# LayerNorm column sums taken from the f32 tile instead of a bf16 copy (gated-scan block, 8 cores)

## What is computed

```
xg    = gelu(x)
for fwd, bwd:                     # the scan runs forwards / backwards in time
    xb = xg @ Wx + bx
    a  = sigmoid(xb @ Wga + bga) * sigmoid(a_logit)
    h  = scan(a, sqrt(1 - a*a) * sigmoid(xb @ Wgx + bgx) * xb)
    y += h @ Wo + bo
r1  = gelu(y/2 + x) @ ld_W + ld_b + x + x
x1  = layernorm(r1)
r2  = x1 + clip((x1 @ sign(W_ffn).T) * scale + bias, -100, 100)
out = layernorm(r2)               # over the 1024 features
```

## Time and profile before

| | us |
|---|---|
| median of 2 runs (757.25 and 760.36) | 758.81 |
| the profiled execution | 756.73 |
| span of its slowest core (core 0) | 755.2 |
| spans of the other cores | 733.6 to 752.3 |
| mean granted TensorE clock of core 0 | 0.939 of 2.4 GHz |

### The profile page before, as it was taken

How to read it: one execution, slowest core, us unless ns; L and a number is a source line. 1 busy time by engine, 2 the same in 40 slices (tenths; PEclk the granted TensorE clock), 3 DMA queues, 4 the chain that set the end, 5 groups by cost and what they waited for, 6 DMA issues and landing times.

```text
span 755.2 us, 7191 instructions; the slowest of 8 cores (733.6 to 755.2 us)
## 1 busy us (share of the span) xinstructions
PE 622.8 (82%) x2667; PEld 263.7 (35%) x2720; DVE 330.6 (44%) x193; ACT 353.6 (47%) x262; POOL 48.7 (6%) x92
## 2 busy tenths in 40 slices
PE   0449999999999999999999979988896798775510
PEld 0014444444444444444444424433332243221100
DVE  0000000005677687677771202032478388475274
ACT  2442332236776877877832201133563467534710
POOL 2010000000000000002032111000000000000000
PEclk9999999999999999999999989999998989887855
DMA  8995000012232222223289999165530000112024
GB/s 186 243 199 98 1 0 1 1 15 33 37 43 42 31 41 43 42 30 55 42 110 195 228 188 183 45 196 187 175 111 1 0 1 1 45 66 112 0 65 158
DMA packets 23218, 61.34 MB, mean 81 GB/s; under 512 B 2704, under 2 KB 2704, under 8 KB 23184
## 3 DMA queue, kind: packets, MB, share of 16 engines
q0 software_dynamic: 12672, 23.07, 21.2%
q1 hardware_dynamic: 8208, 29.42, 12.2%
q10 hardware_dynamic: 2304, 8.39, 3.8%
HBM read 75.55 MB, written 8.39 MB: 111 GB/s over the span
## 4 chain that ended last, share of the span: by engine, by line
PE 64%; DMA 15%; DVE 9%; ACT 6%; issue 4%; SPq 0%; ACTq 0%; DVEq 0%; POOLq 0%
PE psA L152 34%; PE psB L152 30%; DMA A<-x 6%; DMA A<-Wof 3%; DMA A<-Wob 2%; DVE A L719 2%; DMA out<-A 2%; DVE A L783 2%; DMA A<-Wffn 2%; DVE A L712 2%; ACT A L868 1%; DVE A L683 1%; ACT A L778 1%; DVE srows L611 1%; DVE A L690 1%
## 5 line engine op out<-in xcount | busy, mean ns | idle before, releaser
L152 PE MATMUL psA<-A 128*128 128x512 bf16 x1503 | 361.6, 396 | 70.1 <-ACT A L329 22.6
L152 PEld LDWEIGHTS psA<-A 128*128 128x128 bf16 x1536 | 151.4, 100 | 275.4 <-issue 112.4
L152 PE MATMUL psB<-A 128*128 128x512 bf16 x1004 | 226.2, 380 | 1.7 <-DVE A L568 0.6
L152 PEld LDWEIGHTS psB<-A 128*128 128x128 bf16 x1024 | 100.3, 98 | 122.8 <-issue 3.0
L429 DVE TENSOR_SCALAR A<-A,dvec_sb 128x2048 f32<-128x2048 f32 x16 | 20.6, 1286 | 168.8 <-ACT A L425 168.8
L440 DVE TENSOR_TENSOR A<-A 128x2048 f32<-128x2048 f32 x16 | 36.7, 2292 | 51.0 <-ACT A L433 51.0
L573 ACT ACTIVATE A<-A,dvec_sb 128x1024 bf16<-128x1024 f32 x16 | 18.4, 1148 | 75.1 <-DVE A L568 75.1
L425 ACT ACTIVATE A<-psB,vecs_sb 128x2048 f32<-128x2048 f32 x16 | 31.5, 1967 | 32.0 <-PE psB L152 32.0
L152 PE MATMUL psB<-A,ones_sb 128*1 128x512 bf16 x128 | 33.8, 395 | 14.0 <-ACT A L894 11.2
L431 ACT ACTIVATE A<-A 128x2048 f32<-128x2048 f32 x16 | 30.6, 1910 | 23.8 <-DVE A L429 23.8
L568 DVE SCALAR_TENSOR_TENSOR A<-psA,A 128x1024 f32<-128x1024 f32 x8 | 9.8, 1225 | 65.2 <-PE psA L152 37.7
(11 more groups left out here) (54 smaller groups left out, 341.5 us busy)
## 6 DMA issues: line engine op xcount, KB each, us to landing
A<-x SPq DMA_DIRECT2D x40, 512.0 KB, 7.9
A<-x ACTq DMA_DIRECT2D x8, 512.0 KB, 15.3
A<-Wof POOLq DMA_DIRECT2D x16, 256.0 KB, 11.4
A<-Wob POOLq DMA_DIRECT2D x16, 256.0 KB, 13.4
A<-Wffn SPq DMA_DIRECT2D x8, 512.0 KB, 6.1
out<-A ACTq DMA_DIRECT2D x8, 512.0 KB, 4.1
out<-A SPq DMA_DIRECT2D x8, 512.0 KB, 3.9
A<-Wxf POOLq DMA_DIRECT2D x8, 256.0 KB, 31.5
```

The source lines that it names most:

```text
L152: inst = e.matmul(oa, lh, rh, start=st, stop=sp)
```

## The change

In the ffn stage the bf16 copy of r2 is dropped. ACT squares the f32 tile, and the two S1 matmuls of each chunk take the f32 tile as moving operand and a new f32 column of ones as stationary. The squares stay bf16, and so do S2 and the statistics of the ld stage.

```diff
+    ones32_sb = nc.alloc_sbuf_tensor("ones32_sb", [128, 1], F32)
...
+    bd.op("vector", lambda e: e.memset(ones32_sb[:], 1.0), writes=[onesB], inc="dv")
...
-    def stats_tiles(src_ap_fn, src_buf, k, slot):
+    def stats_tiles(src_ap_fn, src_buf, k, slot, f32=False):
+        lh = ones32_sb.ap() if f32 else ones_sb.ap()
         tiles, treads = [], []
         for t in range(2):
-            tiles.append((ones_sb.ap()[:],
-                          src_ap_fn(k, t),
+            tiles.append((lh, src_ap_fn(k, t),
...
         r2B = rA3.new(f"r2h{h}", CH)
-        r2bfB = [new_over(rR1e[k:k + 1], f"r2bfh{h}_{k}") for k in range(CH)]
-        r2bf_ap8 = [A5.ap()[:, R1 // 2 + k * 1024: R1 // 2 + (k + 1) * 1024]
-                    for k in range(CH)]
...
-            bd.op("vector",
-                  lambda e, o=o: e.tensor_copy(r2bf_ap8[o],
-                                               r2f[:, o * 1024:(o + 1) * 1024]),
-                  reads=[r2B[o]], writes=[r2bfB[o]], inc="dv")
-
             def _stats(o=o):
                 sl = o % 2
                 bd.op("scalar",
                       lambda e, o=o, sl=sl:
-                      e.activation(rsq_ap[sl], r2bf_ap8[o], AF.Square),
-                      reads=[r2bfB[o]], writes=[rsqB[sl]], inc="sc")
-                stats_tiles(lambda k, t: r2bf_ap8[k][:, t * 512:(t + 1) * 512],
-                            r2bfB[o], o, 2)
+                      e.activation(rsq_ap[sl], r2f[:, o * 1024:(o + 1) * 1024],
+                                   AF.Square),
+                      reads=[r2B[o]], writes=[rsqB[sl]], inc="sc")
+                stats_tiles(lambda k, t:
+                            r2f[:, k * 1024 + t * 512: k * 1024 + (t + 1) * 512],
+                            r2B[o], o, 2, f32=True)
```

## The result

The changed kernel took 769.83 us (median of 12 runs), the kernel before 758.13 us (median of 10) in the same series. The forecast was 769.3.

A forecast was written before the change was run, and what follows sets the result against it. TensorE was taken to bound the ffn stage's first half and both half-end bursts, DVE's apply steps the second half's first six chunks. +6.1 + 6.25 - 1.8 = +10.5 us on 758.8 gave 769.3 us, range 762 to 784.

The forecast's parts named there:

- The price of an f32 matmul: 32 ones matmuls (S1) in the ffn stage: each four bf16 streams at 2.4 GHz, loads hidden, 0.87 us.
- The bursts: Ones matmuls at each ffn half's end, on which L605 and LayerNorm wait: +6.1 us first half (S(0) included), +6.25 second.
- S(0) of the second half hidden: First chunk's sums in the second half fall into TensorE's 6.45 us wait for ACT's square, so they cost nothing.
- The casts: DVE, second half: three casts off the path before the apply step L712, 3 x 0.61 us, -1.8 us.
- The sum: Both half-end costs less the cast gain: +6.1 + 6.25 - 1.8 = +10.5 us, giving 769.3 us, +1.4%.
- The signs: Profile checks: 32 f32 matmuls of 0.87 us, L605 6 and about 10.5 us later, no 0.6 us step, clock 1.00.
- anything ahead of 626 us moves: Stated failure condition: the prediction is wrong if the profile changes before 626 us, in the ffn stage's first half or earlier.
- The clock in the range: Part of the forecast's own range, 764 to 775: a burst starting at 1.2 instead of 2.4 GHz costs 2 to 3 us.
- The squares from f32, the memset and the new waits at nothing: ACT squares (1048 against 1046 ns), one small DVE memset at 10 us, and waits on finished reads: no cost.
- Exposed loads: Rival, f32 ones matmuls: 83 ns weight load open per stream, 1.20 us per matmul, +20.3 us, 779.1; chance 0.13.
- The fallen clock: Rival, both half-end bursts: TensorE runs at 1.2 GHz during f32 work, +34.7 us, 793.5; chance 0.10.
- Fewer passes: Rival, f32 ones matmuls: each costs one or two bf16 streams, 757.0 or 759.6 us; chance 0.10.

The follow-up runs named there:

- e_sq32: Changed kernel with the squares f32 too, so the matmuls that sum the squares also read f32 (64 f32 matmuls); 788.20 us, 1.0393 to the kernel before.
- e_castback: Changed kernel with the 16 casts put back on DVE, their result read by nothing; 769.98 us, ratio 1.0145 to the kernel before.
- e_mix: Kernel before, with f32 S1, no cast and ready sums issued earlier (o = 2, 4, 6) in the second half; first-half squares read f32; 751.60 us, 0.9895.
- e_hi16: Changed kernel with S1 as bf16 matmuls reading the upper 16 bits of each f32 in place, no cast; 756.46 us, 0.9963 to the kernel before.
- e_f32_h1: Changed kernel with the ready S1 and S2 sums issued earlier, at o = 2, 4, 6, in the second half only; 753.55 us, 0.994 to the kernel before.
- e_best: Kernel before (bf16 S1) with the sums issued earlier in both halves and three second-half copies moved to ACT; 748.21 us, 0.9858 to the kernel before.

## Why the prediction was right, point by point

- *The price of an f32 matmul*, taken as four bf16 streams at 2.4 GHz, 0.87 us: measured 0.86, in the changed kernel and in e_sq32. By the rule of the Trainium skill ("FP8 and Floating Point Precision", section on TensorE precision notes), four passes, it would be 4 x 0.217 = 0.87; the trace agrees in time, though it shows two records and not four.
- *The bursts*: +6.1 and +6.25 forecast. Measured +1.28 for S(0) in the first half (2.24 instead of 0.96 us between the two chunks' matmuls) and +4.52 for the burst, 5.8 together; +6.15 in the second. The first was 0.3 too long, 0.2 of it because I had S2(2) wait for its square, when S1(2) was still running.
- *S(0) of the second half hidden*: right, it lies at 695.16 in front of a wait of 5.63 us.
- *The casts*: this term was mis-sized. Forecast 3 x 0.61 = 1.8 us; by e_castback they are worth 3 x 0.80 = 2.4, and the steps shrank by another 0.35 that is not theirs. I had taken the step from the cast's start to the apply's start. But the apply starts 0.08 us before the residual add's end (672.64 + 1.22 = 673.86 against 673.78), where the cast had started 0.1 us behind it: consecutive DVE instructions overlap at their ends, and a removed one takes its gap along.
- *The sum*: forecast +10.5; the stage's stretches give +9.55, the timed runs +9.5 to +13.4. What the timed median has over the stage's stretches, some 2 us, lies within that interval, and no part of it could be placed. The terms are right to within 1 us each. That the times came out as close as 769.8 for 769.3, and 767.28 for 767.2 in the profiled execution, is luck: what the stage gave less was made up outside it.
- *The signs*: L607 of the first half came 9.5 us after the L605 of before and that of the second 12.9, where 6 and 10.5 were forecast. By the sign "anything ahead of 626 us moves" the prediction would be wrong, since the slowest core reached the stage 4.0 us later. The sign was too sharp for one execution against another; counted from the first Relu pass it is 5.5 and 9.0. The other signs came out, with 64 records where 32 matmuls were expected.
- *The clock in the range*: a burst's start at 1.2 GHz was taken at 2 to 3 us. No row showed that, and where it happened it was less: 1.2 us between the two bursts of the kernel before (6.66 and 5.43 us for 22 matmuls), 1.46 us in e_mix.
- *The squares from f32, the memset and the new waits at nothing*: the square takes 1049 ns, and with e_hi16, which has all three, the time is under that of before.
- *Exposed loads* are out: their bound was 1.2 us a matmul, and the spacing is 0.43 per record with the 0.08 us load inside it. *The fallen clock* is out for this kernel: 1.00 through both bursts. *Fewer passes* is out by the spacing; its side, that nothing is lost, was reached by e_f32_h1 in another way, through the place of the work and not its price.

## What to carry to other kernels

An f32 matmul in place of a bf16 one costs as much as three more of the same, 0.65 us at 512 columns here, although its stationary operand is a single column; other widths were not run. Against a cast of 0.69 us for two of them on another engine it pays only where TensorE waits anyway. So price it by place: the 16 f32 matmuls of the second half cost 5.7 us in a burst on which a LayerNorm waited, and 0.5 us where 12 of them stood in TensorE's idle time for DVE. Before trading work between engines, look whether work that is deferred to the end of a stage has a wait earlier in the stage that could hold it: with the bf16 sums that gave 1.4% (e_best), and with the f32 sums, moved in one half, it turned 1.5% above the kernel before into 0.6% below it.

## What was not expected of the hardware

- An f32 matmul stands in the profile as two records of 0.43 us each, so counts of instructions double without a change in the program (64 for 32).
- A bf16 operand read with a step of two elements (the upper halves of f32 values) ran at the pace of a dense one: in e_hi16 S1(1), S2(1) and S1(2), four such matmuls and two dense ones, took 1.49 us, six dense ones 1.45.
- The clock's fall is not told by the wait before it alone. It was at 1.2 GHz after waits of 2.25, 2.32 and 2.48 us, and stayed at 2.4 GHz after waits of 1.97 and 2.60 us. The same 2.25 us stood before the second burst of the kernel before, where the clock was 1.00 from 706 to 708. In e_castback the 16 matmuls of chunk 6 took 3.61 us behind a wait of 3.29 us on core 7, and 5.30 us behind one of 2.11 us on core 1. Some 0.7 to 1.5 us of path hung on it where a burst or a pair waited for these matmuls, and nothing where they had slack.
- DVE had an idle time of 0.46 us without a releaser at about the same instruction of its list (the 172nd to 174th that the profile has) in three kernels, whatever stood there. By where it fell it cost 0.35 us, or nothing.
